# Retention block with a top-2 mixture of experts: expert rows added in DRAM onto rows that hold x, and a tail with four normalised buffers and a projection added straight from PSUM

## What is computed

```python
def reference(x, ...):
    xn = _layernorm(x)
    return x + attention(xn) + experts(xn)

def attention(x):                  # 16 heads of 16, decaying causal scores, no softmax
    attn = einsum('bihd,bjhd->bhij', q, k) * decay[None] / scale
    y = einsum('bhij,bjhd->bihd', attn, v)
    yn = (y - mean over tokens and head channels) / sqrt(var + EPS)
    yn = yn.reshape(b, t, dm) * gn_weight + gn_bias
    return yn @ W_o.T

def experts(x):                    # 8 experts, each token goes to 2 of them
    probs = softmax(x_flat @ gate_w.T + gate_b)
    topk_vals, topk_idx = top_k(probs, 2)
    h = relu(x @ w1[e] + b1[e]); y = h @ w2[e] + b2[e]
    return sum over the token's two experts of topk_val * y
```

## Time and profile before

| | |
|---|---|
| median of 3 runs | 878.24 us (877.22 to 878.96) |
| the profiled execution, its own time | 879.42 us |
| its span in the profile | 877.6 us |
| mean granted TensorE clock | 0.973 of full speed |
| busy: PE, DVE, ACT, POOL | 815.5, 687.6, 605.6, 393.5 us |
| HBM read, written | 115.88 MB, 33.18 MB |
| last layer-2 matmuls end | 823.24 us of the span |
| last sum on DVE ends | 871.86 us |

### The profile page before, as it was taken

One profiled execution on the slowest core, in us unless ns is written; L12 is line 12 of the kernel. 1 busy time (PEld: TensorE's weight loads), 2 busy tenths in 40 slices (PEclk: granted clock), 3 DMA queues, 4 the chain that ended last, 5 costly groups with the idle time before them and its releaser, 6 DMA issues.

```text
span 877.6 us, 21858 instructions
## 1 busy us (share of the span) xinstructions
PE 815.5 (93%) x6976; PEld 779.2 (89%) x6976; DVE 687.6 (78%) x1195; ACT 605.6 (69%) x1073; POOL 393.5 (45%) x368
## 2 busy tenths in 40 slices
PE   3947999999999999989999999999999999999864
PEld 1436999999999998989999999999999999999854
DVE  6687888888988889877777777777877777777496
ACT  3824666676757676868777788777788777787631
POOL 2207677777777775113333223333223333223264
PEclk9968999999999999999999999999999999999977
DMA  9923222222222215746666666666666667665587
GB/s 297 365 105 118 84 68 84 72 78 70 80 72 78 66 61 186 285 169 222 240 239 241 232 210 218 244 238 244 228 218 216 238 238 241 233 212 201 163 285 246
DMA packets 85769, 162.08 MB, mean 185 GB/s; under 512 B 26672, under 2 KB 56752, under 8 KB 75760
## 3 DMA queue, kind: packets, MB, share of 16 engines
q1 hardware_dynamic: 78928, 143.08, 48.0%
q0 software_dynamic: 6816, 18.69, 6.0%
HBM read 115.88 MB, written 33.18 MB: 170 GB/s over the span
## 4 chain that ended last, share of the span: by engine, by line
PE 87%; DVE 7%; issue 2%; DMA 2%; ACT 1%; POOL 0%; SPq 0%; DVEq 0%; ACTq 0%
PE ps L692 28%; PE ps L899 26%; PE ps L810 12%; PE ps L748 5%; PE ps L782 3%; PE ps L758 3%; PE ps L955 2%; PE ps L884 2%; PE ps L767 2%; PE ps L710 1%; PE ps L797 1%; DMA xn<-x 1%; PE ps L834 1%; PE ps L702 1%; PE ps L739 1%
## 5 line engine op out<-in xcount | busy, mean ns | idle before, releaser
L692 PE MATMUL ps<-arena_r 128*128 128x256 f32 (+1 forms) x2064 | 262.3, 285 | 0.4 <-ACT xn L591 0.4
L692 PEld LDWEIGHTS ps<-arena_r 128*128 128x128 f32 x2064 | 250.8, 192 | 4.8 <-issue 0.6
L899 PE MATMUL ps<-arena_r 128*128 128x256 f32 x1872 | 232.6, 284 | 0.9 <-DVE gn_t L1315 0.9
L899 PEld LDWEIGHTS ps<-arena_r 128*128 128x128 f32 x1872 | 228.9, 193 | 0.9 <-issue 0.9
L477 POOL TENSOR_TENSOR fence_out<-eps_col 128x1 f32<-128x1 f32 x39 | 77.7, 1991 | 304.4 <-DVE arena_f L1245 304.4
L537 ACT ACTIVATE arena_r<-arena_f 128x2048 fp32r<-128x2048 f32 x78 | 145.4, 1916 | 0.0
L625 ACT ACTIVATE arena_f<-ps,arena_f 128x256 f32<-128x256 f32 x156 | 65.4, 470 | 90.5 <-PE ps L899 85.1
L810 PE MATMUL ps<-arena_r 128*128 128x128 f32 x1024 | 120.5, 276 | 0.0
L810 PEld LDWEIGHTS ps<-arena_r 128*128 128x128 f32 x1024 | 116.9, 192 | 0.0
L1261 DVE TENSOR_TENSOR arena_r<-arena_f,arena_r 128x2048 fp32r<-128x2048 f32 x39 | 89.4, 2291 | 34.5 <-ACT arena_r L537 34.5
L544 ACT ACTIVATE arena_r<-arena_f 128x512 fp32r<-128x512 f32 x128 | 77.0, 629 | 48.6 <-DVE arena_f L1146 45.4
(11 more groups left out here) (145 smaller groups left out, 1108.1 us busy)
## 6 DMA issues: line engine op xcount, KB each, us to landing
arena_f<-w SPq DMA_DIRECT2D x78, 1024.0 KB, 5.0
xs_rows<-spare_rows SPq DMA_DIRECT2D x39, 258.0 KB, 3.7
arena_f<-xs_rows SPq DMA_DIRECT2D x39, 258.0 KB, 2.6
pair_chunk<-xn SPq DMA_DIRECT2D x32, 256.0 KB, 2.5
arena_f<-pair_rows SPq DMA_DIRECT2D x16, 512.0 KB, 5.1
arena_f<-b SPq DMA_DIRECT2D x39, 128.0 KB, 3.0
xn<-x SPq DMA_DIRECT2D x8, 512.0 KB, 8.9
x_chunk<-xn SPq DMA_DIRECT2D x32, 128.0 KB, 2.0
```

The costliest lines, as they stand in the source:

```text
L692: last = pe.matmul(out_ap, lhs(a), rhs(b), start=start and n == 0, stop=stop and n == 2, **kw)
L899: last = pe.matmul(ps[:, 2 + hp, o * SLOT:(o + 1) * SLOT], w1_r[par][:, a, at:at + P], xs_r[:, b, k * SLOT:(k + 1) * SLOT], start=(m == 0 ...
```

## The change

`pair_rows` (two rows per token) becomes `sum_rows` (one row per token, and 256 spare rows). Right behind the stores of the spare row pattern SP issues one copy of x from DRAM to DRAM into `sum_rows`, so that each row starts as x. The pair number of a token's pairs becomes the token's number, and the expert scatters add to the row (`compute_op=ALU.add`) where they wrote it. The reads of `pair_rows`, POOL's 16 sums, the four reloads of x and DVE's 16 sums with the experts' rows go; SP reads `sum_rows` in 8 DMAs of 512 KB after the last scatter. The normalised outputs get four buffers, in the weight buffers of odd slots, and the products of PE three places in PSUM. ACT starts its tail after its own work in the last slot, and DVE makes two low halves ahead of the last `ys_gated`.

```diff
-        "pair_no": (np.arange(NT)[None, :, None] * P + i[:, None, None]).repeat(2, 2).reshape(P, -1) * 2.0
-        + np.tile([0.0, 1.0], NT),
+        "token_no": np.arange(NT)[None, :] * float(P) + i[:, None],
...
-    pair_rows = nc.dram_tensor("pair_rows", [2 * NT * P + SLOT, D], F32).ap()
+    sum_rows = nc.dram_tensor("sum_rows", [NT * P + SLOT, D], F32).ap()
...
-        yn_r = fr(2, 2, KC, 4 * P)
+        sums = ff(NT // 4, 4, D)
+        yn_r = [t[:, h * KC * 4 * P * 2:(h + 1) * KC * 4 * P * 2].rearrange("p (s c i) -> p s c i", s=2, c=KC)
+                for t in (w1_r[1].rearrange("p s n -> p (s n)"), w2_r[1].rearrange("p s n -> p (s n)")) for h in range(2)]
...
@@ sync, behind the 39 spare-row stores
+            sp.dma_start(sum_rows[0:NT * P].rearrange("(p t) d -> p (t d)", p=P),
+                         x.rearrange("b (q t) d -> (b q) (t d)", t=NT)).then_inc(s["sums_x"], 16)
             sp.wait_ge(s["rows_done"], 2)
...
@@ sync, tail
-            tokens_load(3, NS - 1)
-            tokens_load(2, NS - 1)
-            slot_step(NS - 2, NS % 2)
-            tokens_load(0, NS)
-            tokens_load(1, NS)
...
-            for q in range(4):
-                pair_rows_load(q)
+            for hb in range(NT // 4):
+                sp.dma_start(sums[:, hb], sum_tiles[:, hb * 4:hb * 4 + 4, :]).then_inc(s[f"sums_in{hb}"], 16)
             for q in range(NT // 2):
                 sp.wait_ge(s["out_sb"], q + 1)
-                if q + 4 < NT // 2:
-                    pair_rows_load(q + 4)
-                sp.dma_start(out_tiles[:, q * 2:q * 2 + 2, :], x_rows(q * 2, 2)).then_inc(s["out_done"], 16)
+                sp.dma_start(out_tiles[:, q * 2:q * 2 + 2, :], sums[:, q // 2, q % 2 * 2:q % 2 * 2 + 2]).then_inc(s["out_done"], 16)
...
@@ gpsimd, rows_scatter
+                pool.wait_ge(s["sums_x"], 16)
...
-                        pair_rows, bass.IndirectOffsetOnAxis(ap=pair_slot[:, par, j:j + 1], axis=0),
-                        ys[:, j * D:(j + 1) * D], None).then_inc(s["pairs_out"], 16)
+                        sum_rows, bass.IndirectOffsetOnAxis(ap=pair_slot[:, par, j:j + 1], axis=0),
+                        ys[:, j * D:(j + 1) * D], None, compute_op=ALU.add).then_inc(s["pairs_out"], 16)
...
-            for q in range(NT // 2):
-                pool.wait_ge(s[f"pair_in{q % 4}"], q // 4 * 16 + 16)
-                nc.gpsimd.tensor_tensor(y_pair[:, q % 4, :, 0], y_pair[:, q % 4, :, 0], y_pair[:, q % 4, :, 1], ALU.add).then_inc(s["y_sum"], 1)
...
@@ scalar, tail
-            act.wait_ge(s["ys_psum"], NS)
+            act.wait_ge(s["ys_psum"], NS - 1)
...
-                wait(act, s["o_psum"], hb - 1)
+                wait(act, s["o_psum"], hb - 3)
...
@@ tensor, tail
-            pe.wait_ge(s["ys_sb"], NS)
+            pe.wait_ge(s["xst_l"], NS)
+            pe.wait_ge(s["h_f"], NS * (FC // 2))
...
-                wait(pe, s["attn_res"], hb - 1)
+                wait(pe, s["out_sb"], 2 * (hb - 2))
...
@@ vector, tail
-            ys_gated(NS - 1, (NS - 1) % 2)
-            ...
-                V.tensor_tensor(half, half, ps[:, par * 2:par * 2 + 2, :].rearrange("p a b -> p (a b)"), ALU.add).then_inc(s["attn_res"], 1)
-                dve.wait_ge(s["attn_res"], hb + 1)
-                for q in (2 * hb, 2 * hb + 1):
-                    dve.wait_ge(s["y_sum"], q + 1)
-                    V.tensor_tensor(x_rows(q * 2, 2), x_rows(q * 2, 2), y_pair[:, q % 4, :, 0], ALU.add).then_inc(s["out_sb"], 1)
+            def out_half(hb):
+                dve.wait_ge(s[f"sums_in{hb}"], 16)
+                dve.wait_ge(s["o_psum"], hb + 1)
+                for q in range(2):
+                    pair = sums[:, hb, q * 2:q * 2 + 2].rearrange("p t d -> p (t d)")
+                    V.tensor_tensor(pair, pair, ps[:, hb % 3 * 2 + q, :], ALU.add).then_inc(s["out_sb"], 1)
+
+            low_half(0)
+            low_half(1)
+            ys_gated(NS - 1, (NS - 1) % 2)
+            low_half(2)
+            low_half(3)
+            for hb in range(2 * B):
+                out_half(hb)
+                if hb + 4 < 2 * B:
+                    low_half(hb + 4)
```

More of the change, by code:

```diff
@@ L120, in build @@
     xs_rows = nc.dram_tensor("xs_rows", [NS * SLOT, W], F32).ap()
-    pair_rows = nc.dram_tensor("pair_rows", [2 * NT * P + SLOT, D], F32).ap()
-    pair_tiles = pair_rows[0:2 * NT * P].rearrange("(t p k) d -> p t (k d)", p=P, k=2)
+    sum_rows = nc.dram_tensor("sum_rows", [NT * P + SLOT, D], F32).ap()
+    sum_tiles = sum_rows[0:NT * P].rearrange("(t p) d -> p t d", p=P)
     x_tiles = x.rearrange("b (c p) d -> p (b c) d", p=P)
@@ L243, in build @@
         w1_r[1], w2_r[1] = fr(2, KC * F), fr(2, FC * D)
-        ff.at = raw_at
-        x_res = [ff(CB, D) for b in range(B - 1)]
         ff.at = 0
-        x_res.append(ff(CB, D))
-        y_pair = ff(4, 2, 2, D)
-        assert ff.at <= raw_at
-        fr.at = 0
-        yn_r = fr(2, 2, KC, 4 * P)
-        def x_rows(tile, count):
-            return x_res[tile // CB][:, tile % CB:tile % CB + count]
+        sums = ff(NT // 4, 4, D)
+        assert NS % 2 == 1
+        yn_r = [t[:, h * KC * 4 * P * 2:(h + 1) * KC * 4 * P * 2].rearrange("p (s c i) -> p s c i", s=2, c=KC)
+                for t in (w1_r[1].rearrange("p s n -> p (s n)"), w2_r[1].rearrange("p s n -> p (s n)")) for h in range(2)]
         y_mv = sb("y_mv", [P, B, KC, 2])
@@ L276, in build @@
             "fence scat0 scat1 r_zero "
-            "gn_chain gn_avg_psum gn_var gn_std gn_ab yn_f yn_h yn_l o_psum x_res_in0 x_res_in1 x_res_in2 x_res_in3 "
+            "gn_chain gn_avg_psum gn_var gn_std gn_ab yn_f yn_h yn_l o_psum sums_x sums_in0 sums_in1 sums_in2 sums_in3 sums_in4 sums_in5 sums_in6 sums_in7 "
             "xs_in0 xs_in1 bias_in0 bias_in1 w1_in0 w1_in1 w2_in0 w2_in1 w1_h w1_l w2_h w2_l xst_psum xst_h xst_l "
-            "h_psum h_f h_h h_l ys_psum ys_sum ys_sb pair_slot pairs_out spare y_sum attn_res out_sb out_done "
-            "pair_in0 pair_in1 pair_in2 pair_in3"
+            "h_psum h_f h_h h_l ys_psum ys_sum ys_sb pair_slot pairs_out spare out_sb out_done"
         ).split():
@@ L953, in out_half @@
                         for k in range(KC):
-                            last = pe.matmul(ps[:, par * 2 + t // 2, t % 2 * D:(t % 2 + 1) * D], yn_r[:, par, a, k, t * P:(t + 1) * P], wo[:, b, k, :],
+                            last = pe.matmul(ps[:, hb % 3 * 2 + t // 2, t % 2 * D:(t % 2 + 1) * D], yn_r[hb % 4][:, a, k, t * P:(t + 1) * P], wo[:, b, k, :],
                                              start=(m == 0 and k == 0 and t % 2 == 0), stop=(m == 2 and k == KC - 1), skip_group_check=True)
                 last.then_inc(s["o_psum"], 1)
-            run_steps(pe, 0, 2 * B, 2, 2 * B, out_half)
+            for hb in range(2 * B):
+                out_half(hb)
         @block.vector
@@ L1325, in _ @@
             run_steps(dve, 2, NS, 2, NS - 1, slot_step)
-            ys_gated(NS - 1, (NS - 1) % 2)
-            def low_half(hb, par):
-                dve.wait_ge(s["yn_h"], hb + 1)
-                wait(dve, s["o_psum"], hb - 1)
-                V.tensor_tensor(yn_r[:, par, 1].rearrange("p c (t i) -> p t c i", t=4), y_t[:, hb * 4:hb * 4 + 4],
-                                yn_r[:, par, 0].bitcast(F32).rearrange("p c (t i) -> p t c i", t=4), ALU.subtract).then_inc(s["yn_l"], 1)
-            def out_half(hb, par):
-                if within(hb + 1, 2 * B):
-                    low_half(hb + 1, 1 - par)
-                half = x_rows(hb * 4, 4).rearrange("p t d -> p (t d)")
-                dve.wait_ge(s[f"x_res_in{hb // 2}"], 16)
-                dve.wait_ge(s["o_psum"], hb + 1)
-                V.tensor_tensor(half, half, ps[:, par * 2:par * 2 + 2, :].rearrange("p a b -> p (a b)"), ALU.add).then_inc(s["attn_res"], 1)
-                dve.wait_ge(s["attn_res"], hb + 1)
-                for q in (2 * hb, 2 * hb + 1):
-                    dve.wait_ge(s["y_sum"], q + 1)
-                    V.tensor_tensor(x_rows(q * 2, 2), x_rows(q * 2, 2), y_pair[:, q % 4, :, 0], ALU.add).then_inc(s["out_sb"], 1)
@@ L1348, in _, with low_half, out_half @@
-            low_half(0, 0)
+            def low_half(hb):
+                dve.wait_ge(s["yn_h"], hb + 1)
+                wait(dve, s["o_psum"], hb - 3)
+                V.tensor_tensor(yn_r[hb % 4][:, 1].rearrange("p c (t i) -> p t c i", t=4), y_t[:, hb * 4:hb * 4 + 4],
+                                yn_r[hb % 4][:, 0].bitcast(F32).rearrange("p c (t i) -> p t c i", t=4), ALU.subtract).then_inc(s["yn_l"], 1)
+            def out_half(hb):
+                dve.wait_ge(s[f"sums_in{hb}"], 16)
[3 more added lines that the diff above has]
+                    V.tensor_tensor(pair, pair, ps[:, hb % 3 * 2 + q, :], ALU.add).then_inc(s["out_sb"], 1)
```

22 lines of the change are left out of this document (7 added, 15 removed).

## The result

The changed kernel takes 863.0 us, the median of 4 runs (861.11 to 864.51), beside 878.6 us for the kernel before (877.22 to 881.59). The ratio is 0.982, with a 95% interval of 0.980 to 0.985: 15.6 us faster. The forecast was 867.7 with a range of 860 to 875.

A forecast was written before the change was run, and what follows sets the result against it. PE, busy for 93% of the span, bounds the kernel except where it stands still, chiefly in a tail bound by DMA and DVE. Tail -14.2 and copy +3.7 make -10.5 us from the median 878.24: 867.7, range 860 to 875.

The forecast's parts named there:

- The copy of x: At the start: DRAM-to-DRAM copy in two passes at 385 GB/s, 21.8 us, done at 71.5, making PE 3.7 us late.
- cost 0: At the start: the copy's lower bound, one pass at 345 GB/s, 12.2 us, done at 61.9 before routing is.
- the copy hides: Rival at the start: the copy goes at a store's rate, ends before 63.5, costs nothing; 864.0 us; chance 0.27.
- a copy that ends before 63: At the start: one of the signs listed as showing the forecast wrong, set against DMA full from 49.7 to near 71.
- The last scatter: In the tail: last gated result 2.6 us later behind two low halves, plus 1.0 for the add; rows complete at 833.1.
- The add: In the tail: adding in the last scatter's flight costs 1.0 us, between bounds of 0 and 3.1; no second issue.
- The DMAs: In the tail: 8.39 MB after the last scatter at 335 GB/s take 25.0 us, from 834.6 to 859.6.
- The end of the program: After the tail's last bytes: 3.8 us to the end of the span, as before, so the span ends at 863.4.
- PE: In the tail: PE stands until about 838.5, then 120 matmuls take 16.9 us to 855.4; DMA ends last.
- The slots: The 38 other scatters cost nothing; two in a slot may take 6.0 us more than now before PE feels it.
- slower: Rival in the slots: adding scatters exceed their 6.0 us and each of 37 slots grows by the excess; chance 0.09.
- The rule from the Trainium skill on adding copies: Last scatter in the tail: adding goes at half rate, doubling the 1.43 us behind the issue; sum 0.4 us higher.

The follow-up runs named there:

- experiment 5: Changed kernel with scatters that write plainly where they added, leaving out the sum of a token's two experts and x: 862.6 us, ratio 0.980.
- experiments 1, 2 and 9: Changed kernel, last gated result behind one low half: 860.1 us; also four PSUM places, all low halves first: 862.1; four places, low halves as in the change: 860.9.

## Why the prediction was right, and where it was off

The direction, the place and the mechanism held: the gain is in the tail, its bulk is 4.19 MB that no longer move behind the last scatter, and DMA ends last. The size was off: a gain of 10.5 us was forecast and 15.6 measured, and the time was 4.7 below the forecast. It comes from these terms.

- **The copy of x: +3.7 forecast, no cost found.** This is the step that failed. I let DRAM give and take each byte in two passes and had 21.8 us. The second of two copies landed 12.7 us behind the first, 330 GB/s, one pass as for the 39 stores. The bound that I had put at "cost 0" was the right one, and the rival "the copy hides" (chance 0.27) came true, but with less to spare than it had: it let the copy end at 61.9, ahead of SP's next issue, and it landed at 64.5, 0.5 behind it. I had named a copy that ends before 63 as a sign of being wrong; that sign is absent, and yet the copy costs nothing. That its 864.0 is within 1.0 of the time is in part luck, since the terms below miss by 1.3 one way and by 1.5 and 2.0 the other. The Trainium skill (DMA: Bandwidth & Descriptors, latency and other measured facts) has 214 GB/s as the full rate of copies between HBM tensors in tiles of 128 partitions by 16 KiB. The trace disagrees for the copy here, with 330.
- **The last scatter: landing forecast at +9.9 us from the last layer-2 matmul, measured +11.2.** The delay by two low halves was forecast at 2.6 and is 2.3 (826.18 against 823.84). The add was put at 1.0, all of it flight and none of it issue; it is 1.5 (experiment 5), of which 0.6 is POOL's longer issue of the first scatter. And POOL's first step in the tail takes 1.23 us beside a low half on DVE where it took 0.19 in the kernel before, when DVE was free.
- **The DMAs: 25.0 us forecast, 23.5 measured,** at 354 GB/s, not 335. Right in kind, and experiments 1, 2 and 9 show that it is this that ends the kernel.
- **The end of the program: 3.8 us kept, 1.8 found.** I carried over the kernel before's time between the last byte and the end of the span as if it were fixed.
- **PE: forecast 120 matmuls in 16.9 us from 838.5, measured 16.3 from 840.6.**
- **The slots: cost 0 forecast and found, by a wrong rule.** The room was not 6.0 us but 1.5 in a cycle, and the price beyond it not the excess but 6.6 us a slot. With the measured landing the kernel was 1.0 to 1.5 us from a loss of 200. A chance of 0.09 for "slower" came from a margin that doesn't exist; that the flight was no longer is luck.

The rule from the Trainium skill on adding copies (Collectives: The Full Stack, why ReduceScatter is half of AllGather: two reads for each write) gave 0.4 more than the forecast. The trace bears it out in kind: from issue to landing 4.3 us against 2.4 without the add, which is 2.7 against 1.4 behind POOL's issue, and 13.5% of the engines' time against 6.1% for the same bytes. Whether two reads for each write or the threefold number of packets makes it, no run here tells.

## What to carry to other kernels

If a tail moves everything after one last write, count the bytes behind it first, and the sums that stand between a read and its store: taking out a third of the bytes and the sums of the experts' rows was worth nearly all of the 15 us, and the new order of the engines around the old bytes was worth nothing, or less. Let nothing stand ahead of the instruction that the transfer waits for, not even work that its engine has time for; one line moved back gives about 2 us. Where a buffer is written, sent and written again, take the slack of the whole cycle and not of one pass, at its longest flight, and ask what else the late work would ask for at the same moment. Take the end of a transfer from its landing and not from a window, above all where packets are large.

## What the runs showed of the hardware

- A copy of 4.19 MB from DRAM to DRAM, 128 rows of 32 KB in 64 packets of 64 KB, landed 15.7 us behind its issue. A second one right behind it landed 12.7 us later: 330 GB/s, as fast as the 39 stores (329).
- An indirect scatter of 128 rows of 1 KB that adds takes POOL 1.56 us to issue instead of 0.98, and 4.3 us from issue to landing instead of 2.4 (medians). All scatters together make 14304 packets with the add and 6816 without, 96 more for each adding one, at 18.69 MB in both: its rows go in packets of 1 KB where the plain one has 4 KB.
- Beside 2 MB of weight loads such a scatter took 9.9 to 11.7 us to land, and 3.8 to 4.7 in the last slots of the same kernel, which have no such loads.
- While the second of two copies of 4.19 MB ran ahead in its queue, one DMA of 1 KB took SP 6.65 us to issue.
- The same POOL instruction of 128 elements takes 0.19 us when DVE is idle, 1.10 to 1.23 beside a low half of 1.22 on DVE, and 2.08 in the slots beside a low part of 2.28 (778.24 in the kernel after).
